# Middle phase: x transposed by strided loads and VectorE, q and k for two chunks at a time and v as three-part fp32r products

## Chip, cores, metric

The kernel runs on one core of a Trainium2 chip. The metric is the device time of one execution in microseconds (us); lower is better. PE is TensorE, ACT is ScalarE, DVE is VectorE, POOL is GpSimd, SP is SyncE.

## The reference, cut to what matters

x has 8192 rows (4 sequences of 2048) of 256 numbers. Three layers follow each other, each with a residual: a mixture of 8 experts with two chosen per row, a linear attention with 16 heads of 16, and the same mixture again.

```python
x = x + 0.5 * ffn(layernorm(x), Wr, W1, W3, W2)
# attention:
Q = (X @ Wq.T); K = (X @ Wk.T); V = (X @ Wv.T)        # heads of 16
KV = einsum('blhd,blhe->blhde', K, V)
KVc = cumsum(KV, axis=1)                              # causal
Y = einsum('blhd,blhde->blhe', Q, KVc)
Y = einsum('hed,blhd->blhe', Bm, Y)                   # Bm = Lm @ Lm.T, Lm lower triangle
x = x + Y @ Wc.T
x = x + 0.5 * ffn(layernorm(x), Wr, W1, W3, W2)
# ffn: logits = x @ Wr, top 2 of 8, place in the expert's list (capacity 2560),
# silu(xe @ W1) * (xe @ W3) @ W2, weighted and added back
```

## The kernel before

Four phases run one after the other, each a block in which every engine runs its own list of instructions in order, held together by semaphores.

**Route** (`route_phase`, the first 148 us or so): the rows are normed, their logits computed and their places in the experts' lists found, in five groups of 8 or 16 tiles of 128 rows (`GROUPS`). In each group VectorE makes the moments and the choice (`choose`, `place_first`, `place_rest`, `pick_cols`), ScalarE norms rows and copies transposes (`front`), GpSimd makes the row marks (`pick_rows`), TensorE transposes, ranks and tabulates. Between groups ScalarE also starts copies of x (`copy_x`), splits weights (`high_w`) and makes one quad's column marks (`pick_cols_by_scalar`, in a scratch tile `far` that lies in `su.raw_qk`). `Setup` prepares the attention's weights on the side: VectorE subtracts their column means (`center`, behind its group 0, signal `centered`), ScalarE keeps the heads' product (`keep_heads`, behind its group 1).

**Experts 1**, **middle**, **experts 2** follow. Experts multiply in fp32r: a number is split into a high part, rounded to fp32r, and the low rest, and `mm3` adds high by high, high by low and low by high. Their x^T is made by strided loads (`e_spread`) and VectorE's transposes of 32x32 blocks (`e_turned`).

**Middle** (`middle_phase`, about 1261 to 1746 us): the 8192 rows are 64 chunks of 128 (`NCH`), in groups of 8 (`MG`), and the engines' programs loop over `STEPS`, with work of several chunks in one step. At step n TensorE does: `project_qk(n+2)` (q and k, transposed, 8 fp32 products of 128 columns, into the bank `qk`), in some steps the ranks of the group before, `project_v(n+2)` (v and part of the logits, 264 columns, into the bank `xv`), `attend_state(n)`, `scores(n+1)`, in some steps `tabulate`, `attend(n)`, `update(n)`, `turn_k(n+2)` (two transposes, into `qk`), `turn_x(n+3)` (two transposes, into `xv`), `project_out(n)`. Each fp32 product shows as two records in the trace. ScalarE copies results out of PSUM (`keep_k`, `keep_v`, `keep_q`, `keep_y`, `keep_krow`, `keep_x`) and norms the rows of the group before (`norm_x2`); VectorE masks the scores (`mask`, four instructions of 512 columns), keeps the state, adds the output to x (`add_out`) and does norms and routing of the group before; GpSimd makes row marks alone. What sets the order is each engine's own written list; an engine whose first instruction waits holds all that stands behind it.

## Time and profile before

| what | value |
|---|---|
| three runs, median (lowest to highest) | 2888.59 us (2888.28 to 2891.92) |
| profiled execution, its own time | 2889.19 us |
| profiled execution, span of the trace | 2887.4 us |
| TensorE busy | 2743.9 us, 95% of the span |
| VectorE busy | 1702.5 us, 59% |
| ScalarE busy | 1311.9 us, 45% |
| GpSimd busy | 1202.6 us, 42% |
| mean granted TensorE clock, share of full | 0.976 |

The profiled execution's own time is 1.8 us more than its span, which is what lies before the first and behind the last instruction. Busy shares are averages over four phases with different limits, so they don't say what an edit in one phase is worth.

### The profile page before, as it was taken

The numbers are of one execution on the slowest core, as the hardware profiler recorded it, in microseconds if no ns is written. First come the engines' busy times: TensorE is split into PE (matmuls) and PEld (weight loads), VectorE is DVE, ScalarE is ACT, GpSimd is POOL, SyncE is SP. The second block draws the span as 40 slices with busy tenths as digits, with TensorE's granted clock in tenths as the row PEclk, the third lists the DMA queues.
The fourth block names the chain that finished last, engine by engine and source line by source line (L and its number), as shares of the span: only waits on it lengthen the run. The fifth ranks groups of instructions, "written<-read, shape, count | busy, mean of one in ns | idle before, by whom it ended". The sixth has DMA issues, their size and how long they took to land.

```text
span 2887.4 us, 56040 instructions
## 1 busy us (share of the span) xinstructions
PE 2743.9 (95%) x18295; PEld 2480.5 (86%) x18295; DVE 1702.5 (59%) x4037; ACT 1311.9 (45%) x2765; POOL 1202.6 (42%) x1550
## 2 busy tenths in 40 slices
PE   4499999999999999989999995999999999999999
PEld 3389899999999989878888884898999998999988
DVE  8754555465555555457878875445555454555554
ACT  5644444454444444334444443444444444444443
POOL 3744444545454545310111122454445454454543
PEclk8699999999999999999999997999999999999999
DMA  8644345353434343221111013434344434434332
...
DMA packets 320886, 233.07 MB, mean 81 GB/s; under 512 B 181296, under 2 KB 292784, under 8 KB 320688
## 3 DMA queue, kind: packets, MB, share of 16 engines
...
q8 instruction: 110, 1.80, 0.3%
q14 instruction: 88, 0.72, 0.1%
...
## 4 chain that ended last, share of the span: by engine, by line
PE 52%; DVE 3%; issue 1%; ACT 0%; DVEq 0%; POOL 0%; DMA 0%; ACTq 0%; POOLq 0%
PE e_ps L106 8%; PE e_ps L107 8%; PE e_ps L108 8%; PE e_psy L1248 5%; PE mi_qk L1534 3%; PE e_psx L1248 3%; PE e_psy L1250 3%; PE mi_sc L1550 2%; PE mi_yo L1570 2%; PE e_psx L1250 2%; PE mi_yo L1597 2%; PE mi_xv L1540 2%; DVE mi_prob L1715 1%; PE mi_kv L1584 1%; PE mi_yo L1561 1%
## 5 line engine op out<-in xcount | busy, mean ns | idle before, releaser
L1367 DVE TENSOR_TENSOR e_hid<-e_ps,e_gate 128x384 f32<-128x384 f32 (+1 forms) x640 | 382.5, 598 | 394.0 <-ACT e_gate L1306 392.7
L1375 DVE TENSOR_TENSOR e_h_lo<-e_hid,e_h_hi 128x384 fp32r<-128x384 f32 (+1 forms) x640 | 385.0, 602 | 257.3 <-ACT e_h_hi L1310 257.3
L1306 ACT ACTIVATE e_gate<-e_ps 128x384 f32<-128x384 f32 (+1 forms) x640 | 335.4, 524 | 441.1 <-PE e_ps L108 427.7
L1310 ACT ACTIVATE e_h_hi<-e_hid 128x384 fp32r<-128x384 f32 (+1 forms) x640 | 357.2, 558 | 360.8 <-DVE e_hid L1367 348.8
L106 PE MATMUL e_ps<-e_xT_hi,c_wa 128*128 128x384 f32 (+1 forms) x1280 | 448.9, 351 | 5.6 <-issue 5.3
L107 PE MATMUL e_ps<-e_xT_lo,e_wb 128*128 128x384 f32 (+1 forms) x1280 | 450.6, 352 | 0.0
L106 PE MATMUL e_ps<-e_xT_hi,e_wb 128*128 128x384 f32 (+1 forms) x1280 | 450.5, 352 | 0.0
L108 PE MATMUL e_ps<-e_xT_hi,e_wb 128*128 128x384 f32 (+1 forms) x1280 | 450.5, 352 | 0.0
L107 PE MATMUL e_ps<-e_xT_lo,c_wa 128*128 128x384 f32 (+1 forms) x1280 | 448.4, 350 | 0.0
L108 PE MATMUL e_ps<-e_xT_hi,c_wa 128*128 128x384 f32 (+1 forms) x1280 | 448.2, 350 | 0.0
L467 POOL DMA_INDIRECT c_xrow<-normed_rows,e_token x320 | 352.4, 1101 | 153.3 <-POOL e_token L1133 77.9
L1140 POOL DMA_INDIRECT x<-e_yrow,e_y_token x163 | 277.7, 1704 | 298.7 <-DVE e_yrow L1391 248.1
L1140 POOL DMA_INDIRECT out<-e_yrow,e_y_token x163 | 276.8, 1698 | 298.7 <-DVE e_yrow L1391 232.4
L106 PEld LDWEIGHTS e_ps<-e_xT_hi,c_wa 128*128 128x128 f32 x1280 | 241.4, 189 | 21.9 <-issue 7.1
L106 PEld LDWEIGHTS e_ps<-e_xT_hi,e_wb 128*128 128x128 f32 x1280 | 240.3, 188 | 17.3
L108 PEld LDWEIGHTS e_ps<-e_xT_hi,e_wb 128*128 128x128 f32 x1280 | 240.2, 188 | 16.3
L107 PEld LDWEIGHTS e_ps<-e_xT_lo,e_wb 128*128 128x128 f32 x1280 | 240.3, 188 | 15.8
L108 PEld LDWEIGHTS e_ps<-e_xT_hi,c_wa 128*128 128x128 f32 x1280 | 241.2, 188 | 13.8
L107 PEld LDWEIGHTS e_ps<-e_xT_lo,c_wa 128*128 128x128 f32 x1280 | 241.4, 189 | 13.3
L341 POOL TENSOR_SCALAR mi_r_picked_row<-c_steps,mi_r_rowf 128x128 f16<-128x128 f16 x112 | 65.2, 607 | 400.7 <-DVE mi_r_colf L325 400.7
L1248 PE MATMUL e_psy<-e_wb,e_h_hi 128*128 128x512 f32 x640 | 227.7, 391 | 0.0
L1248 PE MATMUL e_psy<-c_wa,e_h_hi 128*128 128x512 f32 x640 | 227.7, 391 | 0.0
...
## 6 DMA issues: line engine op xcount, KB each, us to landing
c_raw<-w SPq DMA_DIRECT2D x544, 64.0 KB, 2.6
...
```

Of the source, the lines that this page charges most:

```text
L106: pe.matmul(out, a[0], b[0], start=first, stop=False)
L107: pe.matmul(out, a[0], b[1], start=False, stop=False)
L108: return pe.matmul(out, a[1], b[0], start=False, stop=last)
L467: pool.indirect_dma_start(self.xrow[:, sub, :], None, xn, bass.IndirectOffsetOnAxis(ap=token[:, sub:sub + 1], axis=0), bounds_check=ROWS - ...
L1140: pool.indirect_dma_start(acc, bass.IndirectOffsetOnAxis(ap=y_token[:, sub:sub + 1], axis=0), yrow[:, sub, :], None, bounds_check=ROWS - 1 ...
L1248: pe.matmul(bank[:].rearrange("p (u d) -> p u d", u=2), h[0][:, f, own], both[:, :, at:at + D], start=(f == 0), stop=False)
L1250: return pe.matmul(bank[:, D:2 * D], h[1][:, f, own], both[:, 0, at:at + D], start=False, stop=(f == KF - 1))
L1306: act.activation(gate[:, f % 2, 0:n], ps1[f % 2][:, 0:n], ACT.Silu).then_inc(gated, 1)
L1310: act.activation(h[0][:, f, 0:n], hid[:, f % 2, 0:n], ACT.Copy).then_inc(h_high, 1)
L1367: dve.tensor_tensor(hid[:, f % 2, 0:n], ps3[f % 2][:, 0:n], gate[:, f % 2, 0:n], ALU.mult).then_inc(hid_ready, 1)
L1375: dve.tensor_tensor(h[1][:, f, 0:n], hid[:, f % 2, 0:n], h[0][:, f, 0:n].bitcast(F32), ALU.subtract).then_inc(h_ready, 1)
L1534: ins = pe.matmul(qk[:, blk * P:(blk + 1) * P], k.wqk[:, kk, blk * P:(blk + 1) * P], xT[n % 2][:, kk, :], start=(kk == 0), stop=(kk == KD ...
```

## The change

**Setup.** The centred weights of q, k, v and of the router are kept as a high and a low part in fp32r. `split_high` (ScalarE, behind its group 0) waits for `centered` 1; `split_low` (VectorE, behind its group 1) signals `centered` 2. `keep_heads` and `pick_cols_by_scalar` now wait for `centered` 2. The raw weights of v, Wc and the heads' product lie in the experts' tile `xrow`. The rows of the weights are loaded in another order, which is the one that the strided loads give.

**Middle.** x^T is made for pairs of chunks: SyncE issues four strided loads from DRAM (`spread_rows`), VectorE transposes 32x32 blocks (`square`, 128x512), ScalarE rounds the high part (`high_x`), GpSimd subtracts to get the low part (`low_x`). TensorE no longer transposes x. q of a pair is 12 fp32r products of 256 columns (`project_q`, odd steps), k likewise (`project_k`, even steps), v of a chunk is 6 of 264 columns and stands between `update` and `project_out`. `turn_k(n+1)` stands behind `scores(n+1)` and goes to the bank `xv`. The mask is two instructions of 1024 columns.

```diff
@@ -602,9 +602,21 @@
         k = self.k
         dve.wait_ge(self.means_made, 1)
         for kk in range(KD):
-            dve.tensor_tensor(k.wqk[:, kk, :], self.raw_qk[:, kk, :], self.pm[:, 0:2 * D], ALU.subtract)
-            ins = dve.tensor_tensor(k.wvr[:, kk, :], self.raw_vr[:, kk, :], self.pb[:, 0:WV], ALU.subtract)
+            dve.tensor_tensor(self.raw_qk[:, kk, :], self.raw_qk[:, kk, :], self.pm[:, 0:2 * D], ALU.subtract)
+            ins = dve.tensor_tensor(self.raw_vr[:, kk, :], self.raw_vr[:, kk, :], self.pb[:, 0:WV], ALU.subtract)
         ins.then_inc(self.centered, 1)
+
+    def split_high(self, act):
+        k = self.k
+        act.wait_ge(self.centered, 1)
+        act.activation(k.wqk[0][:], self.raw_qk[:], ACT.Copy)
+        act.activation(k.wvr[0][:], self.raw_vr, ACT.Copy).then_inc(self.heads_ready, 1)
+
+    def split_low(self, dve):
+        k = self.k
+        dve.wait_ge(self.heads_ready, 1)
+        dve.tensor_tensor(k.wqk[1][:], self.raw_qk[:], k.wqk[0][:].bitcast(F32), ALU.subtract)
+        dve.tensor_tensor(k.wvr[1][:], self.raw_vr, k.wvr[0][:].bitcast(F32), ALU.subtract).then_inc(self.centered, 1)
 
...
     def keep_heads(self, act):
-        act.wait_ge(self.heads_made, 1)
-        act.activation(self.bbd[:], self.pb[:, 0:KD * P].rearrange("p (a n) -> p a n", a=KD),
+        act.wait_ge(self.heads_made, 2)
+        act.wait_ge(self.centered, 2)
+        act.activation(self.bbd, self.pb[:, 0:KD * P].rearrange("p (a n) -> p a n", a=KD),
                        ACT.Copy).then_inc(self.heads_ready, 1)
-        act.wait_ge(self.heads_made, 2)
         act.activation(self.wc_ext[:, :, D:WV], self.pm[:, 0:KD * E].rearrange("p (a n) -> p a n", a=KD),
                        ACT.Copy).then_inc(self.heads_ready, 1)
 
...
                     else:
                         r.weigh(act, g, chunks(g))
+                    if g == 0:
+                        su.split_high(act)
                     if g == 1:
                         su.keep_heads(act)
...
-                            act.wait_ge(su.centered, 1)
+                            act.wait_ge(su.centered, 2)
                             r.pick_cols_by_scalar(act, g, g % 2, quad(g, i), i, far)
                 su.keep_fold(act)
...
                     if g == 0:
                         su.center(dve)
+                    if g == 1:
+                        su.split_low(dve)
                 r.read_counts(dve)
...
+                def spread_rows(p):
+                    wait(sp, x_squared, p)
+                    for j in range(QUARTERS):
+                        rows = x1_in[p * 2 * P:(p + 1) * 2 * P, j * KD * SQ:(j + 1) * KD * SQ]
+                        sp.dma_start(spread[j * SQ:(j + 1) * SQ, :, :],
+                                     rows.rearrange("(u s) d -> s u d", s=SQ)).then_inc(x_spread, 16)
+
+                for n in STEPS:
+                    if pair_at(n + 6) is not None:
+                        spread_rows(pair_at(n + 6))
...
+                def low_x(p):
+                    pool.wait_ge(x_high, p + 1)
+                    pool.tensor_tensor(xT[p % 2][1][:], turned[:], xT[p % 2][0][:].bitcast(F32),
+                                       ALU.subtract).then_inc(x_low, 1)
+
+                for n in STEPS:
+                    g, c = divmod(n, MG)
+                    if pair_at(n + 4) is not None:
+                        low_x(pair_at(n + 4))
+                    if c in (4, 5) and 1 <= g < MGS:
+                        r.pick_rows(pool, g - 1, (g - 1) % 2, MQ * (g - 1) + c - 4, c - 4)
...
-                def project_qk(n):
-                    pe.wait_ge(xT_ready, n + 1)
-                    wait(pe, kr_kept, n)
-                    for blk in range(2 * KD):
+                def wqk(kk, blk):
+                    return tuple(part[:, kk, blk * P:(blk + 1) * P] for part in k.wqk)
+
+                def project_q(p):
+                    pe.wait_ge(x_low, p + 1)
+                    wait(pe, qk_kept, 2 * p)
+                    for blk in range(KD):
                         for kk in range(KD):
-                            ins = pe.matmul(qk[:, blk * P:(blk + 1) * P], k.wqk[:, kk, blk * P:(blk + 1) * P],
-                                            xT[n % 2][:, kk, :], start=(kk == 0), stop=(kk == KD - 1))
+                            ins = mm3(pe, qk[:, blk * 2 * P:(blk + 1) * 2 * P], wqk(kk, blk),
+                                      (xT[p % 2][0][:, kk, :], xT[p % 2][1][:, kk, :]), kk == 0, kk == KD - 1)
                     ins.then_inc(qk_made, 1)
 
+                def project_k(p):
+                    pe.wait_ge(qk_kept, 2 * p + 1)
+                    for blk in range(KD):
+                        for kk in range(KD):
+                            ins = mm3(pe, qk[:, blk * 2 * P:(blk + 1) * 2 * P], wqk(kk, KD + blk),
+                                      (xT[p % 2][0][:, kk, :], xT[p % 2][1][:, kk, :]), kk == 0, kk == KD - 1)
+                    ins.then_inc(qk_made, 1)
+
                 def project_v(n):
+                    high, low = xT[n // 2 % 2]
                     for kk in range(KD):
-                        ins = pe.matmul(xv[:, 0:WV], xT[n % 2][:, kk, :], k.wvr[:, kk, :],
-                                        start=(kk == 0), stop=(kk == KD - 1))
+                        ins = mm3(pe, xv[:, 0:WV], (high[:, kk, own(n)], low[:, kk, own(n)]), (k.wvr[0][:, kk, :], k.wvr[1][:, kk, :]),
+                                  kk == 0, kk == KD - 1)
                     ins.then_inc(v_made, 1)
...
                 def turn_k(n):
-                    pe.wait_ge(q_kept, n + 1)
+                    pe.wait_ge(qk_kept, n // 2 * 2 + 2)
+                    pe.wait_ge(v_kept, n + 1)
                     for half in range(KD):
-                        ins = pe.transpose(qk[:, half * P:(half + 1) * P], kT[n % 2][:, half, :], k.ident[:])
+                        ins = pe.transpose(xv[:, half * P:(half + 1) * P], kT[n // 2 % 2][:, half, own(n)], k.ident[:])
                     ins.then_inc(kr_made, 1)
...
                 for n in STEPS:
                     g, c = divmod(n, MG)
-                    if chunk(n + 2):
-                        project_qk(n + 2)
+                    if pair_at(n + 3) is not None:
+                        project_q(pair_at(n + 3))
+                    if pair_at(n + 2) is not None:
+                        project_k(pair_at(n + 2))
                     if c == 3 and g >= 1:
+                        wait(pe, v_kept, min(n + 2, NCH))
                         r.ranks(pe, g - 1, MG)
-                    if chunk(n + 2):
-                        project_v(n + 2)
                     if chunk(n):
...
-                    if chunk(n + 1):
-                        scores(n + 1)
...
+                    if chunk(n + 1):
+                        scores(n + 1)
+                        if c == 3 and g >= 1:
+                            pe.wait_ge(r.rank_read, g)
+                        if c == TAB and g >= 1:
+                            pe.wait_ge(tab_kept, g)
+                        turn_k(n + 1)
                     if chunk(n):
                         attend(n)
                         update(n)
                     if chunk(n + 2):
-                        turn_k(n + 2)
-                    if chunk(n + 3):
-                        if c == 3 and g >= 1:
-                            pe.wait_ge(r.rank_read, g)
-                        if c == TAB and g >= 1:
-                            pe.wait_ge(tab_kept, g)
-                        turn_x(n + 3)
+                        wait(pe, kr_kept, n + 2)
+                        project_v(n + 2)
                     if chunk(n):
                         project_out(n)
...
+                def high_x(p):
+                    act.wait_ge(x_squared, p + 1)
+                    wait(act, v_made, 2 * p - 2)
+                    act.activation(xT[p % 2][0][:], turned[:], ACT.Copy).then_inc(x_high, 1)
...
                 for n in STEPS:
                     g, c = divmod(n, MG)
...
+                    if pair_at(n + 3) is not None:
+                        keep_q(pair_at(n + 3))
+                    if pair_at(n + 2) is not None:
+                        keep_k(pair_at(n + 2))
+                    if chunk(n + 1):
+                        keep_krow(n + 1)
                     if chunk(n):
                         keep_y(n)
                     if chunk(n + 2):
-                        keep_krow(n + 2)
-                    if chunk(n + 3):
-                        keep_x(n + 3)
+                        keep_v(n + 2)
+                    if pair_at(n + 4) is not None:
+                        high_x(pair_at(n + 4))
...
-                    for i in range(4):
-                        dve.tensor_tensor(prob[n % 2][:, i], sc[:, i, :].rearrange("p (h t) -> p h t", h=4),
-                                          k.causal[:].unsqueeze(1).broadcast_to([P, 4, P]),
+                    for i in range(0, 4, 2):
+                        dve.tensor_tensor(prob[n % 2][:, i:i + 2].rearrange("p i h t -> p (i h) t"),
+                                          sc[:, i:i + 2, :].rearrange("p i (h t) -> p (i h) t", h=4),
+                                          k.causal[:].unsqueeze(1).broadcast_to([P, 8, P]),
                                           ALU.mult).then_inc(prob_ready, 1)
...
+                def square(p):
+                    dve.wait_ge(x_spread, SPREADS * (p + 1))
+                    wait(dve, x_low, p)
+                    dve.transpose(turned[:].rearrange("p h (u t) -> p u h t", t=SQ),
+                                  spread[:].rearrange("p u (h d) -> p u h d", d=SQ)).then_inc(x_squared, 1)
...
                     last = g == MGS - 1
+                    if pair_at(n + 5) is not None and n > -2:
+                        square(pair_at(n + 5))
```

ScalarE in the middle before: behind a chunk's `mi_krow` it copies x^T, then the next chunk's k, v (`mi_vpad`, `mi_lgx`) and q.

```order
L1640 ACTIVATE mi_xT<-mi_xv 128x256 [waits mi_xt_made]
L1645 ACTIVATE mi_kT<-mi_qk 128x256 [waits mi_qk_made]
L1662 ACTIVATE mi_vpad<-mi_xv,mi_rsq 128x8x2x16 [waits mi_v_made]
L1664 ACTIVATE mi_lgx<-mi_xv 128x8
L1650 ACTIVATE mi_qeo<-mi_qk,c_even 128x2x128
L1651 ACTIVATE mi_qeo<-mi_qk,c_odd 128x2x128
L1652 ACTIVATE mi_qT<-mi_qk 128x256
L1668 ACTIVATE mi_yT<-mi_yo 128x256 [waits mi_y_made]
L1673 ACTIVATE mi_krow<-mi_qk 128x256 [waits mi_kr_made]
```

ScalarE in the middle now, at the end of an even step and the beginning of an odd one.

```order
L1726 ACTIVATE mi_krow<-mi_xv 128x256 [waits mi_kr_made]
L1721 ACTIVATE mi_yT<-mi_yo 128x256 [waits mi_y_made]
L1715 ACTIVATE mi_vpad<-mi_xv,mi_rsq 128x8x2x16 [waits mi_v_made]
L1717 ACTIVATE mi_lgx<-mi_xv 128x8
L1694 ACTIVATE mi_xT_hi<-mi_turned 128x512 [waits mi_v_made,mi_x_squared]
L1703 ACTIVATE mi_qeo<-mi_qk,c_even 128x4x128 [waits mi_qk_made]
L1704 ACTIVATE mi_qeo<-mi_qk,c_odd 128x4x128
```

The copy of x^T (`mi_xT`), which stood ahead of k and v, is gone; the rounding of the high part (`mi_xT_hi`) stands behind the copy of v, right ahead of the copies of the q whose product reads it.

TensorE in the middle before, from k's transposes to the next q and k.

```order
L1591 MATMUL mi_qk<-c_ident,mi_kT 128x128 [waits mi_q_kept]
L1591 MATMUL mi_qk<-c_ident,mi_kT 128x128
L1525 MATMUL mi_xv<-c_ident,c_raw 128x128 [waits mi_v_kept]
L1525 MATMUL mi_xv<-c_ident,c_raw 128x128
L1597 MATMUL mi_yo<-c_fold,mi_yT 128x264 [waits mi_yT_ready]
L1597 MATMUL mi_yo<-c_fold,mi_yT 128x264
L1534 MATMUL mi_qk<-mi_xT,c_wqk 128x128 [waits mi_kr_kept,mi_xT_ready]
L1534 MATMUL mi_qk<-mi_xT,c_wqk 128x128 x7
L1540 MATMUL mi_xv<-c_wvr,mi_xT 128x264 x2
```

TensorE in the middle now, from the products of v to the first of the next pair's q.

```order
L106 MATMUL mi_xv<-c_wvr_hi,mi_xT_hi 128x264 [waits mi_kr_kept]
L107 MATMUL mi_xv<-c_wvr_lo,mi_xT_hi 128x264
L108 MATMUL mi_xv<-c_wvr_hi,mi_xT_lo 128x264
L106 MATMUL mi_xv<-c_wvr_hi,mi_xT_hi 128x264
L107 MATMUL mi_xv<-c_wvr_lo,mi_xT_hi 128x264
L108 MATMUL mi_xv<-c_wvr_hi,mi_xT_lo 128x264
L1650 MATMUL mi_yo<-c_fold,mi_yT 128x264 [waits mi_yT_ready]
L1650 MATMUL mi_yo<-c_fold,mi_yT 128x264
L106 MATMUL mi_qk<-mi_xT_hi,c_wqk_hi 128x256 [waits mi_qk_kept,mi_x_low]
L107 MATMUL mi_qk<-mi_xT_lo,c_wqk_hi 128x256
```

Between the last product of v and the first of q there are only the two products of the output, and q's first product now waits for `mi_x_low` beside `mi_qk_kept`.

ScalarE in the route phase before, from `keep_heads` of group 1 to the column marks.

```order
L624 ACTIVATE r_su_bbd<-r_pb 128x256 [waits r1_su_heads_made]
L627 ACTIVATE r_su_wc_ext<-r_pm 128x2x8 [waits r1_su_heads_made]
L813 DMA x<-x 128x8x256 x2
L817 ACTIVATE c_wa<-c_raw 128x512 [waits c_raw_loaded0]
L817 ACTIVATE c_wa<-c_raw 128x512 [waits c_raw_loaded1]
L817 ACTIVATE c_wa<-c_raw 128x512 [waits c_raw_loaded2]
L817 ACTIVATE c_wa<-c_raw 128x512 [waits c_raw_loaded3]
L366 ACTIVATE r_su_raw_qk<-c_steps,r_r_colf 128x160 [waits r1_r_tabled,r1_r_placed,r1_su_centered]
```

ScalarE in the route phase now, the same place.

```order
L637 ACTIVATE c_xrow<-r_pb 128x256 [waits r1_su_centered,r1_su_heads_made]
L639 ACTIVATE r_su_wc_ext<-r_pm 128x2x8
L825 DMA x<-x 128x8x256 x2
L829 ACTIVATE c_wa<-c_raw 128x512 [waits c_raw_loaded0]
L829 ACTIVATE c_wa<-c_raw 128x512 [waits c_raw_loaded1]
L829 ACTIVATE c_wa<-c_raw 128x512 [waits c_raw_loaded2]
L829 ACTIVATE c_wa<-c_raw 128x512 [waits c_raw_loaded3]
L366 ACTIVATE r_su_raw_qk<-c_steps,r_r_colf 128x160 [waits r1_r_tabled,r1_r_placed,r1_su_centered]
```

VectorE in the route phase now, the end of its group 1 and the beginning of group 2.

```order
L352 TENSOR_SCALAR r_r_picked_col<-c_steps,r_r_colf,c_code 128x160 [waits r1_r_tabled,r1_r_placed]
L352 TENSOR_SCALAR r_r_picked_col<-c_steps,r_r_colf,c_code 128x160 x7
L618 TENSOR_TENSOR c_wqk_lo<-r_su_raw_qk,c_wqk_hi 128x1024 [waits r1_su_heads_ready]
L619 TENSOR_TENSOR c_wvr_lo<-c_xrow,c_wvr_hi 128x528
L238 TENSOR_SCALAR r_r_lg<-r_lg 128x128 [waits r1_lg_made]
```

`keep_heads` waits for `centered` too, and what raises it to 2 stands on VectorE behind all column marks of group 1; everything behind it in ScalarE's list, group 3's norms included, comes after it.

## Rows read from the trace of the kernel before

**Rows 1.** Waits of VectorE, 1345 to 1462 us: total, times, longest.

```profile
DVE mi_prob L1715 <- PE mi_sc L1550: 10.3, 8, 3.1
```

**Rows 2.** Waits of TensorE, 1300 to 1700 us, same columns.

```profile
PE mi_yo L1561 <- DVE mi_x L1737: 1.2, 3, 0.4
```

**Rows 3.** Timeline of TensorE, one chunk of the middle: start us, us.

```profile
1405.54 1.95 PE L1534 MATMUL mi_qk<-mi_xT,c_wqk 128*128 128x128 f32 x16
1407.32 1.06 PE L1540 MATMUL mi_xv<-c_wvr,mi_xT 128*128 128x264 f32 x4
1408.21 0.61 PE L1561 MATMUL mi_yo<-mi_qT,mi_state 128*128 128x128 f32 x4
...
1411.60 0.38 PE L1525 MATMUL mi_xv<-c_ident,c_raw 128*128 128x128 f32 x2
1411.82 1.06 PE L1597 MATMUL mi_yo<-c_fold,mi_yT 128*128 128x264 f32 x4
1412.71 1.95 PE L1534 MATMUL mi_qk<-mi_xT,c_wqk 128*128 128x128 f32 x16
```

**Rows 4.** Timeline of TensorE in an expert: fp32r products.

```profile
804.93 0.39 PE L1248 MATMUL e_psy<-c_wa,e_h_hi 128*128 128x512 f32 x1
805.16 0.28 PE L1250 MATMUL e_psy<-c_wa,e_h_lo 128*128 128x256 f32 x1
...
813.26 0.34 PE L106 MATMUL e_ps<-e_xT_hi,c_wa 128*128 128x384 f32 x1
```

**Rows 5.** Timeline of ScalarE in the middle, behind one v product.

```profile
1408.41 0.47 ACT L1662 ACTIVATE mi_vpad<-mi_xv,mi_rsq 128x256 f32<-128x256 f32 x1 [0.51 <-PE mi_xv L1540]
...
1408.85 0.48 ACT L1650 ACTIVATE mi_qeo<-mi_qk,c_even 128x256 f32<-128x256 f32 x1
```

**Rows 6.** Tile c_wa: count, min/median/max ns, of ScalarE and GpSimd.

```profile
L817 ACT ACTIVATE c_wa<-c_raw x12: 612/614/632, 66.8 to 117.4; 128x512 fp32r<-128x512 f32 x12
L927 POOL TENSOR_TENSOR c_wa<-c_raw,c_wa x6: 1265/1276/1295, 80.5 to 134.2; 128x512 fp32r<-128x512 f32 x6
```

**Rows 7.** Timeline of VectorE in the middle: the mask, then the state.

```profile
1418.42 2.48 DVE L1715 TENSOR_TENSOR mi_prob<-mi_sc,c_causal 128x512 f32<-128x512 f32 x4
1420.82 0.41 DVE L1724 TENSOR_TENSOR mi_state<-mi_kv,c_same_head 128x256 f32<-128x256 f32 x1
```

**Rows 8.** Tile e_turned: VectorE's transposes, min/median/max ns.

```profile
L1350 DVE STREAM_TRANSPOSE e_turned<-e_spread x272: 430/435/442, 198.4 to 2871.8; 128x256 f32<-128x256 f32 x136
```

**Rows 9.** Timeline of four engines in the route phase.

```profile
63.75 0.38 ACT L624 ACTIVATE r_su_bbd<-r_pb 128x256 f32<-128x256 f32 x1 [0.87 <-PE r_pb L614]
...
74.89 2.06 ACT L791 ACTIVATE r_xn<-r_xin,r_n_shift,r_n_rstd 128x256 f32<-128x256 f32 x4
...
67.43 7.04 DVE L352 TENSOR_SCALAR r_r_picked_col<-c_steps,r_r_colf,c_code 128x160 f16<-128x160 f16 x24
...
110.75 0.29 DVE L296 TENSOR_TENSOR r_r_pos<-r_rank,c_region 128x128 f32<-128x128 f32 x1 [7.09 <-PE r_rank L290]
...
114.03 18.91 POOL L341 TENSOR_SCALAR r_r_picked_row<-c_steps,r_r_rowf 128x128 f16<-128x128 f16 x32 [6.66 <-DVE r_r_colf L325]
```

**Rows 10.** Timeline of TensorE at the start of the middle phase.

```profile
1262.88 3.48 PE L1534 MATMUL mi_qk<-mi_xT,c_wqk 128*128 128x128 f32 x16 [0.70 <-ACT mi_xT L1640]
```

**Rows 11.** Tile e_spread: its DMA issues on SyncE, min/median/max ns.

```profile
L1107 SPq DMA_DIRECT2D e_spread<-c_xrow x1248: 585/600/2359, 185.4 to 2856.5; - x179
```

**Rows 12.** The page: copies of 64 KB: count, size, us to landing.

```profile
c_raw<-w SPq DMA_DIRECT2D x544, 64.0 KB, 2.6
```

**Rows 13.** Timeline of TensorE at the middle's end: two idle times.

```profile
1733.13 0.91 PE L1561 MATMUL mi_yo<-mi_qT,mi_state 128*128 128x128 f32 x4 [2.55 <-DVE mi_x L1737]
...
1741.38 0.71 PE L1561 MATMUL mi_yo<-mi_qT,mi_state 128*128 128x128 f32 x4 [2.20 <-DVE mi_x L1737]
```

**Rows 14.** Windows of TensorE, two of them: busy us (x count), then PEclk.

```profile
1734.00:1736.00 2.00, 2.00 (x18) 0.50 0.00 0
1742.00:1744.00 2.00, 2.00 (x49) 1.00 0.00 0
```

153 lines of the change are left out of this document (71 added, 82 removed).

## The prediction

> **What bounds the kernel now.** I read the middle phase first, since most of the diff lies there, and in it the waits of the two busiest engines. TensorE waits 1.2 us in all from 1300 to 1700 us [rows 2], VectorE 10.3 us in two groups of 8 chunks, always for the scores [rows 1]. So TensorE's own work sets the pace, and VectorE has only 10.3/2 = 5.2 us of slack per group. TensorE's timeline of one chunk gives the pace: next q and k 7.17 us later (1405.54 to 1412.71) [rows 3]. The mean clock is 0.976, so the middle runs at nearly full clock. In the route phase I read the order of releases: the norms of one group stand in ScalarE's list behind `keep_heads`, and VectorE later waits 7.09 us for ranks and GpSimd 6.66 us for VectorE [rows 9]. There ScalarE, with what hangs on it, leads, not VectorE.
>
> **The products.** By spacing of starts, a chunk loses 1.78 us for q and k, 0.89 for v and 0.22 for x's transposes, 2.89 in all [rows 3]. It gets 12 fp32r products of 256 columns (24 for two chunks) and 6 of 264. In an expert, 24 pairs of a 512- and a 256-column product take 8.33 us, 0.347 a pair; the 512 takes 0.23, the 256 so 0.117 [rows 4]. So q and k cost 12 x 0.117 = 1.40, v 6 x 0.12 = 0.72, together 2.12: **-0.77 us a chunk**. The nearest other row bounds a product from below: 16 records of 128 columns, each with a weight load, 0.111 each [rows 3], hence -0.89; from above I allow 0.13, hence -0.55. The first three steps belong to the start, so 61 steps count: **-47 us** (-54 to -34), if nothing new waits.
>
> **The new wait.** The chain of x^T now runs through three engines. `high_x` stands on ScalarE behind `keep_v` of the step before its reader (second listing), and q's product needs `low_x`, which needs `high_x`; between v's last product and q's first TensorE has only `project_out`, 0.89 us [rows 3]. From the end of v's products: 0.20 until `mi_vpad` starts, 0.44 for it and `mi_lgx` (1408.41 to 1408.85) [rows 5]; `high_x`, 128x512 SBUF to SBUF with rounding to fp32r, 0.61 by ScalarE's same shape; `low_x` 1.28 by GpSimd's [rows 6]; two hand-overs (ScalarE to GpSimd, GpSimd to TensorE) between nothing and the 0.20 seen here, I take 0.08 each, the upper half being pipelined work. Sum 0.20 + 0.44 + 0.61 + 1.28 + 0.16 = 2.69, less 0.89: **1.80 us of stall per pair** (1.64 to 2.04). Nothing else hides it, as everything behind `project_q` waits in TensorE's list: k, the state, and the scores for which VectorE waits. About 30 of 32 pairs are steady: +54 us (49 to 61). With the -47: **+7 us**, or two steps take 14.34 - 1.54 + 1.80 = 14.60 us for 14.34.
>
> Two smaller terms: in 7 groups `turn_k` now waits behind the scores for VectorE to read the ranks, where `turn_x` did so several products later; no row shows that wait, I bound it by 0 and 0.7 us each and take +2 in all. At the end, TensorE already waits 2.55 and 2.20 us for VectorE [rows 13], and a stall or so is lost in that slack: -2.
>
> **VectorE.** The mask's four instructions took 2.40 us, 0.60 each [rows 7]; two of 1024 columns save at most two starts, and I take 2.27. A square of 128x512 is twice the shape that takes 0.435 [rows 8]; between that and 0.87 I take 0.65, +0.32 a chunk. Net +0.19 a chunk, 1.5 us a group, against 5.2 us of slack [rows 1]: nothing as long as TensorE stalls. The strided loads are four issues of about 0.6 us a pair on SyncE's queue [rows 11], which has 14 us for them; their landing is asked for only some steps later: nothing.
>
> **The start of the middle.** The first product came at 1262.88, behind a copy of x^T [rows 10]. Now there lie ahead of it four issues (2.4 us) [rows 11], a landing (2.6, by copies of 64 KB) [rows 12], square 0.65, high 0.61, low 1.28 [rows 6], 7.5 us. What goes are two transposes (0.22) [rows 3], a 256-column copy (0.48) [rows 5] and their hand-overs (0.2 each), 1.3; a load of x stood there before too, but how much of it was waited for no row shows, so below I allow half of the new landing. 7.5 - 1.3 = 6.2. q and k of the first pair then share one bank and take turns with ScalarE's copies, little more: **+6** (3 to 10).
>
> **The route phase.** `keep_heads` now waits for `centered` 2. What raises it stands on VectorE behind the column marks of group 1, which start at 67.43 and take 7.04 [rows 9], so end at 74.5; `split_low`, 1024 and 528 columns at the mask's 0.60 per 512 [rows 7], takes 1.8: 76.3. Before, `keep_heads` ran at 63.75. Behind it stand two issues of x, four roundings and the norms of group 3, whose start came 11.14 us later (74.89) [rows 9]. At the same distance they start at 87.4 instead of 74.89, some 12 us later. Those norms feed transposes, logits, ranks; VectorE waited 7.09 us for ranks at 110.75, and GpSimd, with 18.91 us of row marks ahead of the tables, 6.66 us for VectorE [rows 9]. So none of these has slack that would take the delay in: **+12** (9 to 14; `split_high` on ScalarE, 1.9 us, may come on top, the issues of x may shrink). The experts start behind the tables, and TensorE is full there, so the delay stays.
>
> **Sum.** +12 + 6 + 7 + 2 - 2 = +25 us. The profiled execution's own time is 2889.19 (its span plus 1.8): 2914.2. The median of the runs shown is 0.6 lower: **2914**. The forecast's own range: 12 (9 to 14), 6 (3 to 10), steady 7 (-5 to +27, both bounds at once), hence about 2897 to 2934 without the far corner.
>
> **Rivals.** 0.2% is 5.8 us, about what a measurement of this kernel can tell from no change.
>
> A. Faster: there is no stall. What decides is the stall s: 18 (start and route) + 30 s - 47 is below zero for s under 0.97 us. For it: GpSimd's record of 1.28 us may hold time that its reader doesn't wait for, and v's copies may end sooner. Against it: s would have to be half of my sum, and `high_x` and `low_x` alone (1.89) exceed the cover by 1.0. At s = 0 TensorE would gain 6.2 us a group, VectorE's slack of 5.2 less 1.5 allows 3.7 only [rows 1]: 8 x 3.7 = 30, -30 + 18 = -12, 2877. Chance 0.08; a stall of 0.78 to 1.16, no change, 0.05.
>
> B. The route's delay is absorbed, because group 3's transposes wait for something else anyhow: 2902. Against it the two waits of [rows 9]. 0.07.
>
> C. Slower still: the clock falls in the stalls. After an idle time of 2.55 us the windows show PEclk at 0.50 (the 1.2 GHz level) at 1734 us; after 2.20 us it stood at 1.00 at 1742 [rows 13, 14]. My stall is shorter than both, and comes every 14.6 us. If it does fall for 3.4 us of work, about half a chunk, each of 30 stalls costs 1.7 more: +51, 2965. 0.10.
>
> D. `low_x` is held up by VectorE. GpSimd's subtractions in the route phase took 1.265 to 1.295 us while VectorE was at work [rows 6], so none is seen to have been held. Where one short VectorE instruction (the state's 0.41 [rows 7], on average partly over, 0.3) stood ahead each time: 30 x 0.3 = +9, 2923. 0.15. The Trainium skill, "SBUF — State Buffer", section "Who interferes with whom", says that a VectorE instruction with two SBUF inputs and a GpSimd instruction that reads SBUF exclude each other for the whole instruction; `low_x` has two such inputs, the mask only one (its other lies in PSUM). By that rule D would be how the middle goes whenever a norm's or routing's instruction falls there; the even 1.265 to 1.295 doesn't bear it out.
>
> My forecast itself, with the stall near 1.8: 0.55.
>
> **How the numbers follow.** Forecast 0.55, D 0.15, C 0.10, A 0.08, B 0.07, no change 0.05. The range 2896 to 2932 leaves out A, C, most of no change, and a small edge of the forecast: about 2 in 10. Faster 0.08, same 0.05, slower 0.87 (forecast, B, C, D all lie beyond +5.8).
>
> **What would show it.** A wait of TensorE at `mi_qk` for GpSimd's `mi_xT_lo`, some 30 times, 1.8 us each; a longer or shorter one sizes the stall by itself. Starts of the 256-column products 0.117 us apart. ScalarE at `c_xrow` waiting some 11 us for VectorE's `c_wvr_lo` in the route phase, and the first expert's products 12 us later. The first q product of the middle 6 us later, counted from the phase's beginning. PEclk near 1.00 in the middle. VectorE's waits for scores grown by the stall, not gone. The prediction is wrong if TensorE's wait is under 1 us or for ScalarE alone, if VectorE no longer waits in the middle, if the route's end hardly moves, or if the clock sits at 0.50 in part of the steps.

## The result and the profile after

Four runs of the changed kernel have a median of 2926.57 us (2925.78 to 2928.93), beside 2890.26 for the kernel before in the same comparison. The ratio is 1.0129, 95% interval 1.0117 to 1.0141: slower by about 36 us. The prediction was 2914 with a range of 2896 to 2932; the direction and the range held, and the time lies 12.6 us above the forecast. Times and ratios here are of undisturbed executions alone: two of e3 and one of the kernel before, which took 5.5 to 13.7 thousand us, are left out.

The profiled execution has a span of 2927.1 us, 39.7 more than before; it is the slowest of the four, 2.4 us above their median. TensorE's waits from 1300 to 1700 us, as in [rows 2] (total, times, longest), and TensorE's window of the same stretch (length, busy us and records, PEclk, DMA share, GB/s):

```profile
PE mi_qk L106 <- POOL mi_xT_lo L1553: 41.7, 26, 1.6
```

```profile
1300.00:1700.00 400.00, 358.31 (x4300) 1.00 0.22 62
```

The forecast wait is there, in every pair, and the clock doesn't fall in it. TensorE's timeline over two steps, to lay beside [rows 3] (start, us, what, and in brackets the idle time ahead and its releaser):

```profile
1344.47 1.05 PE L1650 MATMUL mi_yo<-c_fold,mi_yT 128*128 128x264 f32 x4
...
1346.78 0.61 PE L1613 MATMUL mi_yo<-mi_qT,mi_state 128*128 128x128 f32 x4
1347.31 1.15 PE L1602 MATMUL mi_sc<-mi_qeo,mi_kT 32*128 32x256 f32 x16
1348.39 0.44 PE L1644 MATMUL mi_xv<-c_ident,mi_kT 128*128 128x128 f32 x2
...
1350.24 0.37 PE L106 MATMUL mi_xv<-c_wvr_hi,mi_xT_hi 128*128 128x264 f32 x1
...
1351.06 1.05 PE L1650 MATMUL mi_yo<-c_fold,mi_yT 128*128 128x264 f32 x4
1353.71 0.39 PE L106 MATMUL mi_qk<-mi_xT_hi,c_wqk_hi 128*128 128x256 f32 x1 [1.60 <-POOL mi_xT_lo L1553]
...
1355.78 1.15 PE L1602 MATMUL mi_sc<-mi_qeo,mi_kT 32*128 32x256 f32 x16
...
1362.36 1.15 PE L1602 MATMUL mi_sc<-mi_qeo,mi_kT 32*128 32x256 f32 x16
```

From scores to scores the step with the stall takes 1355.78 - 1347.31 = 8.47 us, the one without 6.58; before, each took 7.18. The stall costs 1.89 here, 1.88 in the mean of such steps. ScalarE's chain ahead of such a wait, as [rows 5], and GpSimd's `low_x` over the whole run (min/median/max ns), as [rows 6]:

```profile
1412.05 0.47 ACT L1715 ACTIVATE mi_vpad<-mi_xv,mi_rsq 128x256 f32<-128x256 f32 x1 [0.97 <-PE mi_xv L108]
...
1412.48 0.63 ACT L1694 ACTIVATE mi_xT_hi<-mi_turned 128x512 fp32r<-128x512 f32 x1
```

```profile
L1553 POOL TENSOR_TENSOR mi_xT_lo<-mi_turned,mi_xT_hi x32: 1256/1265/1275, 1280.6 to 1750.0; 128x512 fp32r<-128x512 f32 x32
```

The route phase, ScalarE, then VectorE, then TensorE's first product of the experts, as [rows 9]:

```profile
78.09 0.38 ACT L637 ACTIVATE c_xrow<-r_pb 128x256 f32<-128x256 f32 x1 [12.15 <-DVE c_wvr_lo L619]
...
87.67 2.06 ACT L803 ACTIVATE r_xn<-r_xin,r_n_shift,r_n_rstd 128x256 f32<-128x256 f32 x4
```

```profile
76.17 1.21 DVE L618 TENSOR_TENSOR c_wqk_lo<-r_su_raw_qk,c_wqk_hi 128x1024 fp32r<-128x1024 f32 x1
77.30 0.70 DVE L619 TENSOR_TENSOR c_wvr_lo<-c_xrow,c_wvr_hi 128x528 fp32r<-128x528 f32 x1
```

```profile
159.51 2.79 PE L1247 MATMUL e_psx<-c_ident,c_xrow 128*32 128x128 f32 x48 [9.74 <-DMA c_xrow<-normed_rows,c_slot_token]
```

`keep_heads` waits 12.15 us for `split_low`, and group 3's norms start at 87.67 instead of 74.89. The last group of rows is TensorE from the start of the middle to its end: q and k of pair 0, q of pairs 1 and 2, the scores of chunk 4, the last output (the first answers to [rows 10]).

```profile
1281.90 0.58 PE L106 MATMUL mi_qk<-mi_xT_hi,c_wqk_hi 128*128 128x256 f32 x1 [17.11 <-POOL mi_xT_lo L1553]
...
1286.67 0.39 PE L106 MATMUL mi_qk<-mi_xT_hi,c_wqk_hi 128*128 128x256 f32 x1 [1.84 <-ACT mi_qT L1705]
...
1292.21 0.58 PE L106 MATMUL mi_qk<-mi_xT_hi,c_wqk_hi 128*128 128x256 f32 x1 [2.49 <-POOL mi_xT_lo L1553]
...
1308.58 0.39 PE L106 MATMUL mi_qk<-mi_xT_hi,c_wqk_hi 128*128 128x256 f32 x1 [1.60 <-POOL mi_xT_lo L1553]
...
1325.69 1.15 PE L1602 MATMUL mi_sc<-mi_qeo,mi_kT 32*128 32x256 f32 x16
...
1784.64 1.16 PE L1650 MATMUL mi_yo<-c_fold,mi_yT 128*128 128x264 f32 x4 [0.51 <-ACT mi_yT L1721]
```

The marks of the same kind in the kernel before: first expert product, the q and k of step 1, the scores of chunk 4, the last output.

```profile
147.25 2.79 PE L1231 MATMUL e_psx<-c_ident,c_xrow 128*32 128x128 f32 x48 [9.68 <-DMA c_xrow<-normed_rows,c_slot_token]
...
1281.78 1.95 PE L1534 MATMUL mi_qk<-mi_xT,c_wqk 128*128 128x128 f32 x16
...
1299.35 1.15 PE L1550 MATMUL mi_sc<-mi_qeo,mi_kT 32*128 32x256 f32 x16
...
1744.71 1.16 PE L1597 MATMUL mi_yo<-c_fold,mi_yT 128*128 128x264 f32 x4 [0.50 <-ACT mi_yT L1668]
```

So the 39.7 us of the span are laid down in three places. The first expert product comes 159.51 - 147.25 = 12.3 us later. From it to step 1 of the middle another 26.8 - 12.3 = 14.5 (1308.58 against 1281.78); 1.6 of these are the stall ahead of that product, one of the steady ones. From there to the last output 13.1 more (39.9 at 1784.64 against 1744.71). Nothing is added behind it.

### The profile page after: what moved, and what is told of

It reads as the page before. It is cut to its first block, busy times and chain, and to the rows that moved or that the text cites. A ratio compares the mean times of both kernels' runs of the same rounds, so it can differ in the third digit from the quotient of the medians.

```text
span 2927.1 us, 55506 instructions
## 1 busy us (share of the span) xinstructions
PE 2714.8 (93%) x18039; PEld 2442.7 (83%) x18039; DVE 1720.6 (59%) x3943; ACT 1297.3 (44%) x2607; POOL 1243.6 (42%) x1582
## 4 chain that ended last, share of the span: by engine, by line
PE 49%; issue 4%; POOL 2%; ACT 1%; DVE 1%; DMA 0%; SPq 0%; DVEq 0%; ACTq 0%; POOLq 0%
PE e_ps L106 8%; PE e_ps L107 8%; PE e_ps L108 8%; PE e_psy L1264 5%; PE e_psx L1264 3%; PE e_psy L1266 3%; PE mi_sc L1602 2%; PE mi_yo L1622 2%; PE e_psx L1266 2%; POOL mi_xT_lo L1553 1%; PE mi_qk L106 1%; PE mi_kv L1636 1%; PE mi_qk L108 1%; PE mi_qk L107 1%; PE mi_yo L1650 1%
## 5 line engine op out<-in xcount | busy, mean ns | idle before, releaser
L1407 DVE SCALAR_TENSOR_TENSOR e_yrow<-e_psy,e_y_weight,e_yrow 128x256 f32<-128x256 f32 x160 | 77.4, 483 | 223.2 <-ACT e_yrow L1339 223.2
```

Of the source, the lines that this page charges most:

```text
L1407: ins = dve.scalar_tensor_tensor(yrow[:, sub, :], ybank[sub][:, D:2 * D], y_weight[:, sub:sub + 1], yrow[:, sub, :], ALU.mult, ALU.add)
```

## The experiments

Each was made from the changed kernel, but for e6 and e9, which were made from the kernel before. The eleven came in four batches, on four chips; each ratio is to the kernel before in the same batch.

**e1: `high_x` earlier.** ScalarE's loop, in the step in which it already ran:

```diff
                     if pair_at(n + 2) is not None:
                         keep_k(pair_at(n + 2))
+                    if pair_at(n + 4) is not None:
+                        high_x(pair_at(n + 4))
                     if chunk(n + 1):
                         keep_krow(n + 1)
...
                         keep_v(n + 2)
-                    if pair_at(n + 4) is not None:
-                        high_x(pair_at(n + 4))
```

Expected: 

> high_x moved up in ScalarE's list, from behind keep_v to right behind keep_k of the same step; nothing else differs from the changed kernel. Theory 1 (the stall is only the place of high_x in the list: it waits behind v's copies for nothing): the waits of mi_qk for mi_xT_lo go, 30 times 1.88 us per pair, and the time falls by 45 to 56 us from 2926.6, to about 2877, below the kernel before. Theory 2 (x^T's chain through three engines is too long wherever it starts, or VectorE takes over as the bound): at most 25 us are won, 2900 or more, and the stall stays in part or VectorE stops waiting for the scores.

Measured: 2924.34 us (2922.39 to 2932.72), ratio 1.0117 (1.0099 to 1.0135). The waits for `mi_xT_lo` are gone, and yet only 2 us were won. TensorE's waits and window in 1300 to 1700 us:

```profile
PE mi_yo L1613 <- DVE mi_x L1787: 33.6, 18, 2.5
```

```profile
1300.00:1700.00 400.00, 362.41 (x4217) 0.96 0.21 61
```

33.6 us of a new wait, for VectorE's `mi_x` (the output's bank has to be read before the next `attend_state` writes it), stand where 41.7 stood for GpSimd, and PEclk is 0.96 instead of 1.00. Where the rest goes is seen in TensorE's timeline of one such place, and VectorE's beside it:

```profile
1394.20 1.05 PE L1650 MATMUL mi_yo<-c_fold,mi_yT 128*128 128x264 f32 x4
...
1398.84 0.71 PE L1613 MATMUL mi_yo<-mi_qT,mi_state 128*128 128x128 f32 x4 [2.17 <-DVE mi_x L1787]
1399.48 2.09 PE L1602 MATMUL mi_sc<-mi_qeo,mi_kT 32*128 32x256 f32 x16
```

```profile
1389.86 0.64 DVE L163 BATCH_NORM_AGGREGATE mi_n_mv<-mi_n_stats 128x2 f32<-128x6 f32 x8
...
1394.99 2.34 DVE L1764 TENSOR_TENSOR mi_prob<-mi_sc,c_causal 128x1024 f32<-128x1024 f32 x2
...
1397.59 0.69 DVE L1793 STREAM_TRANSPOSE mi_turned<-mi_spread 128x512 f32<-128x512 f32 x1
...
1398.32 0.46 DVE L1787 SCALAR_TENSOR_TENSOR mi_x<-mi_yo,mi_n_rstd,c_raw 128x256 f32<-128x256 f32 x1
```

VectorE begins the moments of the next group at 1389.86 and is through with them at 1394.99, when the mask starts; the mask, the state and the square stand ahead of `add_out` (1398.32), and TensorE waits 2.17 us for it though the output had been ready since about 1395. Behind the wait the clock is at half (1.2 GHz): the 16 score products take 2.02 us by spacing instead of 1.08.

In the start of the middle the move did win: from the first expert product (157.9 here) to the scores of chunk 4 6.8 us less, 3.7 of them from chunk 1 on, where the stalls of steps 1 and 3 are gone. From chunk 4 to chunk 60 it lost 10.5 (438.6 against 428.1). This profile is of an execution 8 us slower than the median of e1; in e4, with the same steps and a profile at its median, the loss is 7.3. Of a group of 8 chunks (61.3 us in the changed kernel, 63.6 here) the four stalls, 7.5 us, are gone, and 9.9 have come.

A second cost of the move shows beside it. `low_x` now runs when VectorE makes the choice of experts (step 1 of a group). GpSimd's row, then VectorE's first instruction of the choice:

```profile
1366.01 1.26 POOL L1553 TENSOR_TENSOR mi_xT_lo<-mi_turned,mi_xT_hi 128x512 fp32r<-128x512 f32 x1 [12.61 <-ACT mi_xT_hi L1694]
```

```profile
1366.15 1.21 DVE L243 TENSOR_TENSOR mi_r_lg<-mi_lgs,mi_n_rstd 128x64 f32<-128x64 f32 x1
```

The instruction has two inputs in SBUF and ends 0.1 us behind `low_x`, at 1.21 us instead of 0.21. It is so in all six groups from 1300 to 1700 us, and in e4 and e5, and in none of the changed kernel, e7 and e10, where `low_x` meets other instructions and this one takes 0.21. So VectorE is held for 1.0 us in just the step behind which TensorE waits longest (2.2 to 2.5 us). No run isolates how much of that wait comes from it.

My theory 1 fell; the second half of theory 2, VectorE as the next bound, is what the rows show, but not by its total.

**e2: `split_low` earlier**, in VectorE's loop over the groups:

```diff
                     choose(g)
+                    if g == 1:
+                        su.split_low(dve)
                     if g + 2 < GR:
                         statistics(g + 2)
...
-                    if g == 1:
-                        su.split_low(dve)
```

Expected: 

> split_low moved up in VectorE's list of the route phase, from behind the column marks of group 1 to right behind choose of group 1. Theory 1 (ScalarE is led by centered 2 through keep_heads): the norms of group 3 start some 10 to 13 us earlier than 87.67, and the whole is 9 to 12 us faster, about 2916. Theory 2 (the delay is one of the work added to the three engines, or of VectorE): 0 to 3 us won, 2924 or more.

Measured: 2918.92 us (2915.04 to 2919.94), ratio 1.0096 (1.0078 to 1.0114), so 7.7 us faster than the changed kernel. ScalarE's and TensorE's marks:

```profile
79.47 2.06 ACT L803 ACTIVATE r_xn<-r_xin,r_n_shift,r_n_rstd 128x256 f32<-128x256 f32 x4
...
151.83 2.78 PE L1247 MATMUL e_psx<-c_ident,c_xrow 128*32 128x128 f32 x48 [9.57 <-DMA c_xrow<-normed_rows,c_slot_token]
```

`keep_heads` now runs at 69.15, 8.9 us earlier, group 3's norms start 8.2 us earlier and the first expert product 7.7 earlier. Theory 1 (9 to 12 us) held in its mechanism. Its size can't be judged closely: in the seven other kernels with this edit the first expert product comes at 147.3 to 151.5, so e2's mark is the latest of eight, and in e1, with the route phase of the changed kernel, it comes at 157.9 instead of 159.5. `keep_heads` no longer waits for VectorE in e2 (but 1.67 us for TensorE's `r_pm`).

**e3: both.** Expected: 

> Both moves together. If the two causes are apart they add: 45 to 56 and 9 to 12 us, about 2866 (2858 to 2873). If VectorE or the start of the middle limits what is won in the first move, the sum is the same, as the route phase is another phase; a smaller sum would say that the two places are linked.

Measured: the two runs that count are 2914.33 and 2918.59, so there is no interval; 2858 to 2873 is missed by 40 us or more. e1's move is again worth nearly nothing, in a second kernel, and e2's keeps its worth.

**e4: the start**, added to e3. SyncE's two loads of 1 MB are issued at step -4 instead of -6, behind pair 1's strided loads, and ScalarE makes pair 1's high part at step -3:

```diff
-                    if n == -6:
+                    if n == -4:
                         load(1)
                         load(2)
...
                         keep_q(pair_at(n + 3))
+                    if n == -3:
+                        high_x(1)
```

Expected: 

> Both moves, and in the start of the middle the two loads of 1 MB of x issued behind the second pair's strided loads instead of ahead of them, and high_x of pair 1 right behind keep_q of pair 0. Theory 1 (the start costs 14.6 us more than before because pair 1's strided loads lie behind 2 MB of other loads, and pair 1's chain behind v's copies): 2 to 4 us faster than both moves alone. Theory 2 (the start costs that since q and k of a pair take turns in one bank with ScalarE's copies at half clock): under 1 us.

Measured: 2914.01 us (2911.35 to 2915.88), ratio 1.0082 (1.0064 to 1.0100). Against the two runs of e3 the gain can't be told from nothing, so the marks of the trace decide: first expert product, q of pair 0, q of pair 1, scores of chunk 4.

```profile
148.68 2.79 PE L1247 MATMUL e_psx<-c_ident,c_xrow 128*32 128x128 f32 x48 [9.74 <-DMA c_xrow<-normed_rows,c_slot_token]
...
1270.21 0.58 PE L106 MATMUL mi_qk<-mi_xT_hi,c_wqk_hi 128*128 128x256 f32 x1 [16.32 <-POOL mi_xT_lo L1553]
...
1277.45 0.36 PE L106 MATMUL mi_qk<-mi_xT_hi,c_wqk_hi 128*128 128x256 f32 x1
...
1303.32 1.15 PE L1602 MATMUL mi_sc<-mi_qeo,mi_kT 32*128 32x256 f32 x16
```

q of pair 1 now follows 7.2 us behind that of pair 0 without a wait for x^T; in the changed kernel it was 10.3. From the first expert product to the scores of chunk 4 it is 1154.6 us, 1159.5 in e3, 1166.2 in the changed kernel, 1159.4 in e1, 1152.1 before. So this edit by itself is worth 4.9 us there (theory 1 said 2 to 4). Of the 11.6 us won against the changed kernel, 3.8 are the stalls of steps 1 and 3; the other 7.8 lie ahead of the scores of chunk 1 and come from pair 1's lateness and the order of the loads: theory 1. k of pair 0 waits 1.84 us for ScalarE's copies of q in the changed kernel and in e4 alike, so that q and k take turns is a cost that none of the edits touched. What is won is spent again in the steps, which stay as in e1 (chunk 4 to chunk 60 in 435.4 us).

**e5: less for VectorE.** e4, and the column marks of each group's second quad by ScalarE:

```diff
-        by_scalar = (NCH // QUAD - 1,)
+        by_scalar = tuple(range(1, NCH // QUAD, 2))
...
+                    if c == 5 and 1 <= g < MGS:
+                        r.pick_cols_by_scalar(act, g - 1, (g - 1) % 2, MQ * g - 1, 1, far, False)
+                    if c == 6 and 1 <= g < MGS:
+                        r.pick_cols_from(act, MQ * g - 1, far)
```

Expected: 

> The kernel of e4 (both moves, start edited), and in the middle the column marks of each group's second quad made by ScalarE at the ends of steps 5 and 6, as it makes those of the last quad already, so that VectorE has 8 instructions of 0.35 us, 2.8 us, less in a group. Theory 3 (with the stall gone VectorE is the bound: its step holds back the bank of the output, TensorE waits 2.0 to 2.6 us for mi_x and its clock falls behind such waits): the waits for mi_x shrink, the mean PEclk of the middle rises from 0.96 to nearly 1.00, a group of 8 chunks falls from 62 to about 56 us, and the time from 2914 to about 2870, below the kernel before. Theory 4 (the place of the products themselves or the clock, whatever VectorE does, costs it): at most 10 us won, 2904 or more.

Measured: 2914.09 us (2911.69 to 2916.28), ratio 1.0084 (1.0067 to 1.0101): nothing won. Waits and window:

```profile
PE mi_yo L1617 <- DVE mi_x L1797: 32.0, 18, 2.5
...
1300.00:1700.00 400.00, 364.52 (x4228) 0.96 0.22 63
```

So VectorE's total is not it: with 2.8 us a group less the waits are the same 18. They stand behind `add_out` of VectorE's steps 1, 2 and 5 of a group (in TensorE's list, steps 2, 3 and 6), right behind the moments (steps 0 and 4) and the choice of experts (step 1), not behind the column marks. One of them in TensorE's timeline of e5:

```profile
1424.08 0.88 PE L1617 MATMUL mi_yo<-mi_qT,mi_state 128*128 128x128 f32 x4 [2.46 <-DVE mi_x L1797]
1424.89 2.09 PE L1606 MATMUL mi_sc<-mi_qeo,mi_kT 32*128 32x256 f32 x16
```

Behind this wait of 2.46 us the score products run at half clock (2.09 instead of 1.15). Behind one of 1.43 at 1414.53 they run at full clock, behind one of 1.78 at 1543.13 at half again.

**e6: the kernel before with the same relief.** Expected: 

> The kernel before with only the same relief of VectorE. If VectorE bounds only once the products are shorter (theory 3), this changes little here, as TensorE waits for it 1.2 us in 400: 0 to 6 us faster than 2889, from the few waits. If the relief is worth 20 us or more here too, theory 3 is wrong about where VectorE bounds, and what e5 wins has nothing to do with the change.

Measured: 2887.20 us (2885.56 to 2889.11), ratio 0.9991 (0.9981 to 1.0000), 1.8 us faster than the kernel before: as expected.

**e7: e5 with the stall.** Expected: 

> The kernel of e5 with high_x left where the change has it, behind keep_v (the other edits kept, but for the early high_x of pair 1). Theory 3: the stall of 1.88 us a pair stays and sets the pace, a group takes 60 to 60.7 us as in the changed kernel, the time is 2906 to 2914, and the early high_x, worth 2 us without relief, is worth 35 us or more with it. Theory 4: e7 and e5 differ by under 10 us.

Measured: 2914.37 us (2913.46 to 2915.33), ratio 1.0085 (1.0068 to 1.0102), with 41.7 us waited for `mi_xT_lo` and PEclk 1.00. The time is what theory 3 said of e7 to 0.4 us, but e5 wins nothing over it (0.3 us), so the pair of them goes against theory 3 as I had put it, and meets the bound of theory 4 (under 10 us).

**e8: VectorE's bursts spread.** e5, and the same work in other steps:

```diff
-                    if c < 4 and 0 <= g < MGS - 1:
-                        stats_x1(g + 1, 2 * c)
-                        stats_x1(g + 1, 2 * c + 1)
-                    if c == 4 and 0 <= g < MGS - 1:
-                        moments_x1(g + 1)
+                    if c in (2, 3) and 0 <= g < MGS - 1:
+                        for i in range(6) if c == 2 else (6, 7):
+                            stats_x1(g + 1, i)
+                    if c in (4, 5) and 0 <= g < MGS - 1:
+                        moments_x1(g + 1, 0, MG, c - 4)
+                    if c in (4, 5, 6) and 1 <= g < MGS - 1:
+                        r.pick_cols(dve, g - 1, (g - 1) % 2, MQ * (g - 1), 0, *((0, 1), (1, 2), (2, QUAD))[c - 4])
```

Expected: 

> The kernel of e5, and in the middle VectorE's extra work of a group spread more evenly over its 8 steps: the moments of x1 in two parts (steps 4 and 5 instead of all in 4), the statistics of x1 in steps 2 and 3 instead of 0 to 3, the column marks in steps 4, 5 and 6. No instruction is added or dropped. Theory 3b (what holds TensorE is not VectorE's total but a burst of 5 us in one step, behind which the output's bank comes free 1.4 to 2.5 us late, and the clock falls after the longer ones): the wait of step 5 goes and those of steps 1 and 2 shrink by 0.7 us or more, waits for mi_x from 5.8 to under 2.5 us a group, PEclk over 0.98, a group 62 to about 57 us, time 2914 to about 2875. Theory 4 (the products at their new places cost it, VectorE's order doesn't matter): within 8 us of 2914.

Measured: 2897.07 us (2894.20 to 2898.66), ratio 1.0024 (1.0013 to 1.0035): 17 us faster than e5 with the same instructions (1.0084 to 1.0024 in the ratios). Waits and window, and the longest wait that the timeline shows there with what follows it:

```profile
PE mi_yo L1625 <- DVE mi_x L1805: 20.1, 18, 1.8
PE mi_xv L401 <- DVE mi_r_picked_col L359: 4.4, 6, 0.8
PE mi_xv L1656 <- DVE mi_r_pos L303: 4.0, 6, 0.8
...
1300.00:1700.00 400.00, 371.22 (x4400) 0.99 0.22 64
```

```profile
1419.39 0.71 PE L1625 MATMUL mi_yo<-mi_qT,mi_state 128*128 128x128 f32 x4 [1.83 <-DVE mi_x L1805]
1420.04 1.15 PE L1614 MATMUL mi_sc<-mi_qeo,mi_kT 32*128 32x256 f32 x16
```

The waits for `mi_x` fell from 32.0 to 20.1 us and the longest from 2.5 to 1.8; behind the one shown the scores take 1.15, and PEclk is back at 0.99. The gain is beyond the 8 us of theory 4, so theory 3b held in kind, but the time fell by 17 us of the 39 that I gave, a group takes 60.5 us instead of 57, and the wait of step 5 shrank from about 1.9 to 0.8 and didn't go. A wait for the column marks and one for the ranks (4.4 and 4.0) came up in the place of some of it.

**e9: the kernel before, relieved and spread.** Expected: 

> The kernel before with the same relief (e6) and the same spreading, nothing of the change. Theory 3b: TensorE was held 1.2 us in 400 here, its steps of 7.18 us leave room for a burst, so 2883 to 2889. A gain of 15 us or more would say that the bursts cost the kernel before too.

Measured: 2885.67 us (2883.84 to 2887.41), ratio 0.9985 (0.9975 to 0.9995). It is the lowest time of the study, 4.3 us below the kernel before in its batch (2889.93); against e6 (0.9991) it can't be told from the same.

**e10: e8 with the stall.** Expected: 

> The kernel of e8 with high_x left behind keep_v, as the change has it. Theory 3b: the stall sets the pace again, 2905 to 2914, so that it costs 30 us or more against e8 where it cost nothing before the spreading. Theory 4: within 8 us of e8.

Measured: 2916.34 us (2910.01 to 2919.37), ratio 1.0087 (1.0070 to 1.0104). TensorE waits 41.8 us for `mi_xT_lo` again and for nothing else. The stall sets the pace again, at a time above the 2905 to 2914 and at a cost under the 30 us that I gave. So the same move of `high_x` is worth 2 us in the changed kernel, nothing in e7 and e5, and 19 us in e10 and e8.

**e11: the square behind `add_out`**, added to e8, and four statistics a step earlier:

```diff
-                    if pair_at(n + 5) is not None and n > -2:
-                        square(pair_at(n + 5))
...
                         add_out(n)
+                    if pair_at(n + 5) is not None and n > -2:
+                        square(pair_at(n + 5))
+                    if chunk(n):
                         stats_x2(n)
```

Expected: 

> The kernel of e8, and VectorE's square behind add_out instead of ahead of it, and four of the eight statistics of x1 one step before the group instead of in its steps 2 and 3. Theory 3b: the square's 0.63 us no longer stands between the products of the output and the release of their bank, so the waits for mi_x fall from 20 us in 400 to about 12 or less and the time by 6 to 12 us, to 2885 to 2891, level with the kernel before. If the waits stay and the time moves by under 3 us, what is left of them comes from the bursts of steps 0 and 1 alone.

Measured: 2889.06 us (2885.20 to 2894.42, 11 runs), ratio 0.9996 (0.9987 to 1.0005), 8 us below e8 and in the range given. TensorE's waits, which stayed above the 12 us given, and one of them in its timeline:

```profile
PE mi_yo L1625 <- DVE mi_x L1805: 15.1, 18, 2.1
```

```profile
1362.51 1.23 PE L1625 MATMUL mi_yo<-mi_qT,mi_state 128*128 128x128 f32 x4 [1.82 <-DVE mi_x L1805]
1363.66 2.09 PE L1614 MATMUL mi_sc<-mi_qeo,mi_kT 32*128 32x256 f32 x16
```

Here half clock follows a wait of 1.82 us, as long as the one in e8 that full clock followed. 11.4 of the 15.1 us are such waits, one a group, behind the choice of experts (VectorE's step 1), in which `low_x` again holds an instruction for 0.8 us; behind the moments 0.2 to 0.6 us are left, six times.

The change's products, with their cost taken out of the way, are level with the kernel before and not below it: TensorE still waits 15.1 us in 400 for VectorE, and the start is a few us longer. Beside e9, the kernel before with the same relief and nearly the same spreading (ratio 0.9985), they are level or a little slower; the intervals overlap.

## Why the prediction was right, and where it was off

**Direction and place: right.** The three terms of the sum all showed at their places. In order:

- **Route, +12 predicted, +12.3 measured.** The steps of the working (marks end, `split_low`, distance to group 3's norms) stand in the rows: 76.17 + 1.21 + 0.70, then 78.09, then 87.67. That the size came out to 0.3 us is luck in part: `split_low` began 1.7 later than the 74.5 of the working, and the distance behind it was 9.6 instead of 11.1. e1's route phase, the same, was 10.7 longer than before. e2 undid 7.7.
- **The stall, 1.80 predicted, 1.88 measured.** From `mi_vpad` to `mi_xT_hi` 0.43, `mi_xT_hi` 0.63, `low_x` 1.27: the chain as it was written. It showed 26 times in 400 us.
- **The products, -0.77 a chunk predicted, -0.60 measured.** This term was mis-sized. The 256-column products follow at 0.117 us, as taken from [rows 4]; but twelve of them and the output take 1346.78 - 1344.47 = 2.31 us, where 0.89 + 1.40 = 2.29 was priced, and v's six take 0.82, not 0.72, since the first of a row takes 0.20 or more (`mi_xv` at 1350.24, the output at 1351.06). And `turn_k`, which I took to be moved at no cost, takes 0.37 behind the scores where it took 0.22 behind `update` (`update` itself takes 0.07 less than before). Over 61 chunks this is 10 us.
- **The steps in all, +7 predicted, +13.1 measured.** The stall gave +2, the products +10. Against that, what tables and ranks add is less: over chunks 4 to 60 a chunk takes 7.374 us before and 7.644 after, so above the plain steps (7.18; 7.52) 0.19 and 0.12, 4 us in all; and no wait for the ranks shows ahead of `turn_k`, which I had put at 2.
- **The start, +6 predicted, +14.5 measured.** This step failed. The first product was 6.8 later (6.2 in the working), so that part held. The sentence behind it, that q and k of the first pair "take turns with ScalarE's copies, little more", was small for k of pair 0, which waited 1.84 us for the bank, and left out pair 1: its square waited 2.06 us for loads that lie behind 2 MB of others, its `high_x` stood behind v's copies, and TensorE waited 2.49 us for it, with half clock from there to the scores of chunk 0 (2.09). At the scores of chunk 1 the start is 12.1 us behind the kernel before; e4 took 7.8 of it away. VectorE's square of pair 1 in the start:

```profile
1286.78 0.71 DVE L1793 STREAM_TRANSPOSE mi_turned<-mi_spread 128x512 f32<-128x512 f32 x1 [2.06 <-DMA mi_spread<-x]
```

**Rival A was priced wrong.** It said that without a stall the time would be about 2877. e1 took the stall away and gave 2924. (The prediction also read [rows 1] as all of VectorE's waits there. The same view has 2.3 us more, for the output, so the slack was 6.3 us a group and not 5.2; that makes the price no better.) The slack of 5.2 us a group [rows 1] is an average over eight steps: a burst of 5 us in one step, behind steps now 0.60 shorter, outlasts what TensorE can run ahead, which is limited by one bank of the output. That it is the burst and not the total is what e5 (less work, nothing won) and e8 (the same work spread, 17 us won) show together. To the burst of step 1 the move itself adds 1.0 us, as shown in e1; the prediction had nothing of this. Whether the spreading would do as much without the relief wasn't tried.

**Rival B** is out by the route's 12.3. **Rival C** didn't come where I had put it: PEclk is 1.00 over 400 us with 26 stalls of 1.6 us. Its mechanism came with VectorE's waits in e1, e5 and e11, but the length of a wait doesn't settle it: half clock followed waits of 1.78 (e5), 1.82 (e11), 2.17 (e1) and 2.46 us (e5), full clock waits of 1.83 (e8), 1.92 (e1) and 2.46 us (e4). The 26 stalls of 1.6 us were all followed by full clock, in the changed kernel, e7 and e10 alike. So the stall at 1.88 us was in fact the cheaper wait: VectorE caught up behind it, and the clock stayed. e1 traded it for waits of nearly the same total (33.6 and 4.0), with a clock of 0.96 on top, and so won nothing in the steps. The Trainium skill, "TensorE: Matmul & The Clock Gate", Part 1, says that the array falls to 1.2 GHz when it has been idle and goes back when it has been busy; the rows agree in kind (2.09 us behind a wait, 1.15 again in the next steps). **Rival D** is out for the changed kernel: all 32 `low_x` took 1256 to 1275 ns. The exclusion that the Trainium skill, "SBUF — State Buffer", section "Who interferes with whom", states does show in the experiments, the other way round: where `low_x` was under way first, it was VectorE that stood, 1.21 us for 0.21 (e1). In the changed kernel `low_x` falls on the statistics, which have one input and keep their 0.43 us.

**What stays open**: how much of e11's wait behind the choice is work left over from the moments of step 0 (VectorE has no idle time between the two); what of e1's loss `low_x` causes by holding VectorE; and which of TensorE's waits the clock falls behind.
